# A conditional channel mix and a 6-bit linear layer on one core: the first loads issued in another order from two queues

## What is computed

```python
# x (64, 64, 1024) f32; W (16, 64, 64) f32; condition (64,) int32 in 0..15
y = jnp.einsum('bct,bcd->bdt', x, W[condition])          # a 64x64 mix of channels for each batch entry
p = qweight.reshape(N, 256, 3)                           # 1024 rows of 768 int32 words
v = [p[:, :, 0] & 63, p[:, :, 0] >> 6 & 63, p[:, :, 1] & 63, p[:, :, 2] & 63]   # 4 values of 6 bits
w = (stack(v, axis=2).reshape(N, 1024) - zero_point) * scale
out = x + jnp.einsum('bsk,nk->bsn', y, w) + bias
```

## Time and profile before

| | |
|---|---|
| median of 3 runs | 285.99 us (285.69 to 287.7) |
| the profiled execution | 285.53 us, of which the span of the page is 283.7 us |
| TensorE busy | 276.5 us, 97% of the span |
| DVE, ACT, POOL busy | 191.6, 83.8, 99.1 us |
| granted TensorE clock | 1.00 |
| DMA | 37.96 MB, mean 134 GB/s |

### The profile page before, as it was taken

The page is one execution under the profiler, slowest core; times in us unless marked ns, Lnnn a source line. Parts: engine busy times, 40 slices in busy tenths (PEclk is TensorE's granted clock), DMA queues, the critical chain, the costliest instruction groups (busy, mean ns, idle before and its releaser), DMA issues.

```text
span 283.7 us, 8499 instructions
## 1 busy us (share of the span) xinstructions
PE 276.5 (97%) x3307; PEld 231.1 (81%) x3307; DVE 191.6 (68%) x261; ACT 83.8 (30%) x169; POOL 99.1 (35%) x41
## 2 busy tenths in 40 slices
PE   6999999999999999999999999999999999999995
PEld 2888887788888887988888888888888888888885
DVE  2898897785566556865559555676667655595554
ACT  3795334232044300633017310443106330060000
POOL 4005903964430444314442444404443044430000
PEclk9999999999999999999999999999999999999999
DMA  7930563456115541355114551144413552101112
GB/s 274 375 120 13 178 230 124 152 158 232 75 74 157 163 178 70 114 158 194 74 74 124 165 210 74 74 155 157 157 68 109 165 203 96 74 37 74 74 74 75
DMA packets 20278, 37.96 MB, mean 134 GB/s; under 512 B 6814, under 2 KB 7070, under 8 KB 20266
## 3 DMA queue, kind: packets, MB, share of 16 engines
q1 hardware_dynamic: 19322, 35.43, 36.4%
q10 hardware_dynamic: 944, 2.38, 2.2%
HBM read 21.02 MB, written 16.78 MB: 133 GB/s over the span
## 4 chain that ended last, share of the span: by engine, by line
PE 95%; DMA 2%; issue 1%; ACT 1%; DVE 0%; SPq 0%
PE o_ps L292 71%; PE y_ps L292 12%; PE y_ps L261 10%; DMA w_sb<-in_L_cond_weights_dram 1%; PE o_ps L261 1%; PE o_ps L274 0%; DMA ids<-in_itok_B_dram 0%; PE o_ps L303 0%; ACT qT L442 0%; PE y_ps L274 0%; SPq L160 0%; PE y_ps L303 0%; ACT y_hi L426 0%; DVE o_sb L621 0%; DVE o_sb L623 0%
## 5 line engine op out<-in xcount | busy, mean ns | idle before, releaser
L292 PE MATMUL o_ps<-qT,y_hi 128*128 128x512 f32 (+1 forms) x448 | 171.5, 386 | 0.6 <-ACT qT L442 0.6
L292 PE MATMUL o_ps<-qT,y_lo 128*128 128x512 f32 (+1 forms) x448 | 171.2, 385 | 0.0
L643 POOL TENSOR_TENSOR resid<-x_sb,bias_bc 128x1024 f32<-128x1024 f32 x32 | 95.8, 3000 | 151.0 <-DVE o_sb L545 130.8
L292 PEld LDWEIGHTS o_ps<-qT,y_hi 128*128 128x128 f32 x448 | 83.6, 188 | 17.5 <-ACT qT L442 0.7
L292 PEld LDWEIGHTS o_ps<-qT,y_lo 128*128 128x128 f32 x448 | 83.7, 188 | 16.8
L537 DVE TENSOR_TENSOR o_sb<-o_ps,scale_bc 128x512 f32<-128x512 f32 x54 | 37.3, 690 | 73.6 <-PE o_ps L292 73.6
L426 ACT ACTIVATE y_hi<-y_ps 128x512 fp32r<-128x512 f32 x56 | 29.4, 611 | 96.6 <-PE y_ps L261 96.2
L545 DVE TENSOR_TENSOR o_sb<-o_sb,resid 128x512 f32<-128x512 f32 x63 | 51.5, 822 | 1.9
L417 ACT ACTIVATE junk<-x_sb 128x1024 bf16<-128x1024 f32 x32 | 33.9, 1058 | 63.8 <-DMA x_sb<-in_x_dram 63.8
L526 DVE SCALAR_TENSOR_TENSOR resid<-zs_bc,ysum,resid 128x1024 f32<-128x1024 f32 x32 | 44.8, 1402 | 0.0
L516 DVE TENSOR_TENSOR y_lo<-y_ps,y_hi 128x512 fp32r<-128x512 f32 x57 | 35.6, 683 | 5.4 <-ACT y_hi L426 5.4
(11 more groups left out here) (44 smaller groups left out, 69.2 us busy)
## 6 DMA issues: line engine op xcount, KB each, us to landing
x_sb<-in_x_dram SPq DMA_DIRECT2D x32, 512.0 KB, 3.4
out_dram<-o_sb SPq DMA_DIRECT2D x63, 256.0 KB, 2.1
q_raw<-in_L_ffn_qweight_dram ACTq DMA_DIRECT2D x6, 384.0 KB, 5.4
w_sb<-in_L_cond_weights_dram SPq DMA_DIRECT2D x63, 16.0 KB, 2.0
q_raw<-in_L_ffn_qweight_dram SPq DMA_DIRECT2D x2, 384.0 KB, 6.4
out_dram<-o_sb SPq DMA_DIRECT2D x2, 128.0 KB, 1.9
ids<-in_itok_B_dram SPq DMA_DIRECT2D x1, 0.2 KB
w_sb<-in_L_cond_weights_dram ACTq DMA_DIRECT2D x1, 16.0 KB, 3.4
```

The source lines that it names most:

```text
L292: last = nc.tensor.matmul(bank, part[:, slot, kt, :], qT[:, kt, col:col + width], start=(kt == 0 and part is y_hi), stop=(kt == KT - 1 and ...
L643: nc.gpsimd.tensor_tensor(resid[:, j % RING, :], x_sb[:, j % RING, :], bias_bc[:], ALU.add).then_inc(xbias_ready, 1)
```

## The change

Block 1 moves from ScalarE's stream to SyncE's. Tile 0's rows are loaded in two halves of 64 rows (256 KB), one from each stream, so tile 0's semaphore `x_loaded[0]` counts 32 for its first load and all waits on it ask for 16 more. Tile 1's weight halves and their entry numbers move from SyncE to ScalarE, behind blocks 2 and 3. Blocks 5 and 7 are issued behind `place_q(0)`. The four first entry numbers are read without bounds. TensorE transposes block 1 where the two matmuls on zeros were, ahead of the mix of tile 0. `place_q(1)` comes ahead of `high` of tile 0, and ScalarE does both halves of that `high`; VectorE's copy is gone.

```diff
-            eng.wait_ge(x_loaded[j % RING], (i + j // RING + 1) * 16)
+            eng.wait_ge(x_loaded[j % RING], (i + j // RING + 1 + (j % RING == 0)) * 16)
...
+        def pick_first(eng, at):
+            return eng.value_load(ids[0:1, at:at + 1])
+
+        def load_x_half(eng, half):
+            rows = slice(half * C, (half + 1) * C)
+            eng.dma_start(x_sb[rows, 0, :], x_rows[rows, :]).then_inc(x_loaded[0], 16)
...
             sp.dma_start(ids[:], cond.rearrange("(a b) -> a b", a=1)).then_inc(ids_loaded, 16)
-            load_x(0, 0)
+            load_q(sp, 1)
+            load_x_half(sp, 0)
             sp.wait_ge(ids_loaded, 16)
-            load_w_half(sp, 0, 0, pick(sp, 0))
+            load_w_half(sp, 0, 0, pick_first(sp, 0))
             load_x(1, 0)
-            load_w(1, 0)
             for n in (4, 6):
...
             transpose_q(0)
-            keep_warm(2)
+            transpose_q(1)
             wait_mix(0, 0)
             mix(0, y_banks[0])
-            transpose_q(1)
             transpose_q(2)
...
-            for n in range(2):
-                load_q(act, n)
+            load_q(act, 0)
+            load_x_half(act, 1)
             act.wait_ge(warm_ready, 1)
             nc.scalar.activation(junk[:, 1, 0:1], warm[:, 0:1], ACT.Copy)
             act.wait_ge(ids_loaded, 16)
-            load_w_half(act, 0, 1, pick(act, 1))
-            for n in (2, 3, 5, 7):
+            load_w_half(act, 0, 1, pick_first(act, 1))
+            for n in (2, 3):
                 load_q(act, n)
+            for half in range(2):
+                load_w_half(act, 1, half, pick_first(act, 2 + half))
             place_q(0)
-            high(0, 0, y_banks[0], range(1))
+            for n in (5, 7):
+                load_q(act, n)
             place_q(1)
+            high(0, 0, y_banks[0])
             place_q(2)
...
-            dve.wait_ge(y_ps_ready, 2)
-            dve.wait_ge(y_hi_ready, 1)
-            nc.vector.tensor_copy(y_hi[:, 0, :, S:2 * S], y_banks[0][1]).then_inc(y_hi_ready, 1)
             low(0, 0, y_banks[0])
```

## The result

The changed kernel took **287.89 us** (median of 9 runs, 287.23 to 288.5), against 285.99 (9 runs, 285.31 to 287.7) for the kernel before on the same chip: a ratio of 1.0059, 95% interval 1.0035 to 1.0083. So it is slower by about 1.9 us, where 0.3 us faster was forecast, and the range ended at 286.7. The profiled execution took 287.23 us, the fastest of the nine, with a span of 285.4, 1.7 above.

What follows compares the result with a forecast made beforehand. TensorE, busy 276.5 of 283.7 us, bounds the kernel, so only its early idle time is open. ScalarE's new order starts `first_quarter` at 9.4 instead of 9.73, other terms 0: 285.99 becomes 285.7, range 284.9 to 286.7.

Steps and rivals of the forecast that it cites:

- The two halves.: Tile 0's rows in two loads: same bytes ahead of its weights, mix starts at 6.9 (6.5 to 7.3); cost or gain 0.
- So, roughly, loads go one after another in the order of their issue: Serving of the first loads: in issue order at some 0.4 MB a microsecond, whichever queue they are in.
- Later loads.: Blocks 4 and 6 sooner, 5 and 7 later; block 5 lands at about 12.5 to 13.0; tile 1's weights hidden; 0.
- microsecond to spare: Slack of tile 1's `low` behind block 5 on VectorE, since TensorE is in `second_quarter` until 15.4.
- my third rival: Queues alternate packets, block 3 lands up to 1 us later: 285.9, nothing gained; 0.20 together with held issues.
- ScalarE's stream: Added issues cost: `place_q(0)` at 6.3, `place_q(1)` at 7.3, `high` ends at 9.35, where before the order ended at 9.69.
- The first rival, held issues: ScalarE's issues of blocks 5 and 7 take 0.8 more, `high` ends 9.9 to 10.1: 286.1 to 286.4; 0.20 with shared queues.
- the one engine without slack: ScalarE, by which the forecast was said to fall most easily; its `high`, ending at 9.35, precedes the products at 9.4.
- Bounds were worth nothing: First picks without bounds save 0.25 us each; 0 for tile 0's weights, but everything behind them on ScalarE comes 0.25 sooner.
- The second rival's mark: Tile 1's rows served ahead of block 2, decided if block 2 lands later than about 8.1: 286.6; chance 0.13.
- the shift of 9.73: Start of `first_quarter`, 9.73 before, taken as the number to forecast; its shift, minus 0.33 us, is the end's shift.
- as long as no later piece becomes late: Condition for the shift of `first_quarter`'s start to be the shift of the end; by the sum nothing further was late.

Runs made afterwards that it cites:

- held rows: SyncE waits for tile 1's mix before issuing tile 2's and 3's rows: changed kernel 286.7 us; with column halves and block 5 on SyncE 285.73; kernel before 286.07.
- the repaired changed kernel: Changed kernel with tile 0's halves by columns, blocks 5 and 6 exchanged, and SyncE waiting for tile 1's mix before tile 2's and 3's rows: 285.73 us.

## Why the prediction was wrong

**"*The two halves.* … Cost or gain: 0."** This is the first step that failed. "Ahead of tile 0's weights stand the same bytes as before" holds, but the sum took bytes at one rate whatever their shape. Windows with loads of 64 rows have the DMA engines just as busy and move 235 to 243 GB/s where those with 128 rows move 393 to 404. Tile 0's weights landed at 7.57 instead of 6.77, the mix started at 7.71 and not at the 6.9 forecast, and `first_quarter` at 10.14 and not 9.4. The halves alone, in the kernel before, cost 2.2 us, by columns 0.9. They are not all of it, though. With 128-row loads in the new order the mix still came at 7.25 to 7.81, and how much of that is block 1's transpose, which ended at 7.14 and 7.20 in two of the runs with columns, and how much the share of the queues ahead of the last weight half, no run separates. Nor was that half issued at 2.62, as the sum has it, but at 3.08 (2.69 with columns), behind two loads in place of one. The Trainium skill states the rate: "SBUF — State Buffer", in "Door 1: The DMA port swizzle" and "Can I just issue two DMAs to hit both halves?", has a transfer to 64 partitions reach half of the 16 ports, so at most half of the bandwidth, and two such transfers at once gain only 6% over one. The windows agree in direction: they have 0.6 of the rate (235 and 243 against 393 and 404), with 128-row loads among those of 64. The sentence that I weighed instead, that such transfers "serialize", gives the order and not the rate, and let the term stand at zero. Why two loads by columns cost 0.9 us where their mix is only 0.28 late, and their span no longer than the kernel before's, stays open; the profiled execution was the fastest of the twelve (285.55), so the trace may not show what the median has.

**"So, roughly, loads go one after another in the order of their issue", and "*Later loads.* … At 0."** The second step that failed. The one-after-another rows are of a stretch in which SyncE's queue moved 43 packets of 0.04 MB, though tile 1's rows had been issued; why it moved no more there, these runs don't show. Later both were full, and they shared. The queues of the changed kernel, 12.5 to 16 us:

```profile
q1 hardware_dynamic: 300, 0.63, 55.4%
q10 hardware_dynamic: 220, 0.58, 48.4%
```

Block 5, issued at 6.30 behind the issues of tile 1's weights, was forecast to land at 12.5 to 13.0 and landed at 15.40, since blocks 4 and 6 and tile 2's rows (16.64) on the other queue were served along with it. So it was 2.4 us behind the later of the two forecast times, which is more than the "microsecond to spare" that the sum gave `low` of tile 1: TensorE waited 0.63 us for it, and tile 1's products started 1.33 us later than before, of which 0.51 came with `second_quarter`. That is the mechanism of my third rival ("the queues share packet by packet"), with the right cause and the wrong place: I priced it at block 3, 285.9, and did not follow it to block 5. The rule that it took from the Trainium skill was right for this stretch: 0.63 and 0.58 MB is near to an even sharing.

**Not in the prediction at all:** TensorE's own code. The delay behind tile 1's second product is not one that I could have read in a wait of the kernel before, since it was hidden there, but the load was to be seen: `q8 instruction`, one packet, at 12.88. In the changed kernel it started at 16.47, and TensorE restarted at 18.83. By start times the stop cost 0.52 us there (+1.33 to +1.85), and even that understates it: had block 5 been in time, TensorE would have come at about 16.5 and stopped for longer. The runs with block 5 on SyncE show just that, 1.44 and 1.27 us. The two causes cover each other, which is why neither whole rows, nor columns, nor block 5 alone brought back more than 0.8 us of median, and why the three edits together (columns, block 5, held rows) brought it from 287.89 to 285.73 (1.6 us by the ratios, 1.0059 and 1.0002), as good as the kernel before. That the held rows removed the stop in two kernels and gained nothing in a third ties it to the DMA queues. How exactly the instruction load's start hangs on them I infer and have not shown: in the kernels that stopped, the last data of ScalarE's queue came between 15.46 and 16.25, in the kernel before at 11.63. The end of that queue is not itself the condition: with held rows the load started at 13.71 and 14.22, while ScalarE's queue moved until 14.53 and 14.78 and SyncE's stood empty. Nor does the record name TensorE as the load's owner: that rests on the 2.4 us and on the place, the same in all five, and on the stop in the loop's first round, which keeps the same distance.

**What held.** Block 1 landed at 4.88 (5.1 forecast), and its transpose ran from 5.96 to 6.58 (6.1 to 6.7) under time that TensorE waited anyway. ScalarE's stream came out as summed: `place_q(0)` at 6.27 (6.3), blocks 5 and 7 issued in 1.07 us (0.95) under it, `place_q(1)` at 7.42 (7.3). The first rival, held issues, did not happen. Then `high` had to wait 0.47 us for the mix, so it was the mix and not ScalarE, "the one engine without slack", that held `first_quarter`. Bounds were worth nothing, as said. The second rival's mark, block 2 later than 8.1, was passed (8.22), though not by its mechanism: tile 1's rows landed at 10.11, behind block 2 and not ahead of it; the slow halves delayed both. Forecasting `first_quarter` and taking "the shift of 9.73" for the shift of the end was the frame in which two of three causes had no place: it covers 0.41 of the 1.95 us. The condition that I had set, "as long as no later piece becomes late", was the one to work out.

**The account.** By the change of start times: 0.41 us at `first_quarter` for the late weights (the half-width loads and the new order) less what ScalarE's new order gave; 0.92 more up to tile 1's products, nearly all block 5; 0.52 at the code's load; 0.1 in small pieces up to 29.2; minus 0.2 in the loop's first round. That makes the span's 1.7, and the medians differ by 1.9.

**A better version?** None was found. The stop of 1.2 us in the loop's first round, which the kernel before has too, was not tried. The two best, the kernel before without bounds (285.69, 0.9987 [0.9967, 1.0008]) and the repaired changed kernel (285.73, 1.0002 [0.9987, 1.0016]), cannot be told from the kernel before.

## What to carry to other kernels

A transfer is priced by its partitions too, not only by its bytes: splitting 128 rows into two loads of 64, on one queue or two, kept the engines busy for some 1.7 times as long per byte here (235 to 243 against 393 to 404 GB/s), while splitting by columns kept the rate. When loads are reordered, follow each of them to its consumer until the queues run empty, not only the first few, and price a load beside a full second queue at half the rate. Look in the queue view for instruction loads and ask by how much they are hidden: a load that started 3 us later had its cost here in matmuls whose operands had long landed.

## What the runs showed of the hardware that I had not expected

- TensorE stopped for 1.27 and 1.44 us in a run of matmuls whose operands were all there, and went on 2.4 to 2.5 us after the start of a 16 KB instruction load, which started at 15.85 and 16.10 us there and at 12.88 in the kernel before. A stop of 1.20 us at 50.30, in the kernel before, ended 2.4 us after another such load. The packet of the load in the changed kernel, 16.4 to 16.5 us, and in the kernel before, 12.8 to 12.9 us (queue, kind, packets, MB, share):

```profile
q8 instruction: 1, 0.02, 67.6%
```

```profile
q8 instruction: 1, 0.02, 67.9%
```

  The Trainium skill, "Runtime: NRT & Kernel Launch", section "Instruction fetch mechanics", has code fetched ahead in blocks of 16 KiB over the engine's own DMA queue, "mostly hidden". The size agrees. Hidden was the load at 12.88 in the kernel before; the one at 16.47 in the changed kernel was not, nor those of the loop's first round in both, by the stops behind them.

- TensorE's clock at the start did not simply follow how long it had waited. It was granted half, 0.50, from 8 to 11 us behind a wait of 1.4 us with block 5 on SyncE, and 0.53 from 11.3 to 14.9 with block 1 issued later; but it was granted 1.00 right through behind the 2.4 us wait of the kernel with its halves by rows on SyncE. What decides it these runs don't show. Where it fell, a late load cost more than its lateness: the mix took 1.99 us for 1.16.
